# Picked experts' tiles in one line of pairs behind the last scan, with shifted rows and rings of eight

## The reference, cut to what matters

```
def step(S, inps):
    rt, kt, vt, dt = inps
    kv = kt[..., :, None] * vt[..., None, :]
    o = jnp.einsum('bhk,bhkv->bhv', rt, S + u[None, :, :, None] * kv)
    S = dt[..., None] * S + kv
    return (S, o)
...
up_r = jnp.einsum('th,reh->tre', xt, routed_up)
act = jax.nn.gelu(up_r, approximate=False) * gate[:, :, None]
routed = jnp.einsum('tre,rhe->th', act, routed_down)
```

## Time and profile before

| what | value |
|---|---|
| median of 3 runs | 5062.5 us |
| the profiled execution, its own time | 5088.27 us |
| span of its trace | 5086.5 us |
| mean granted TensorE clock (share of full speed) | 0.899 |
| busy: TensorE, VectorE, ScalarE, GpSimd | 4041.3, 3733.9, 2719.0, 3369.3 us |

### The profile page before, as it was taken

The page is one execution under the profiler, slowest core; times in us unless marked ns, Lnnn a source line. Parts: engine busy times, 40 slices in busy tenths (PEclk is TensorE's granted clock), DMA queues, the critical chain, the costliest instruction groups (busy, mean ns, idle before and its releaser), DMA issues. The chain is left out here.

```text
span 5086.5 us, 64064 instructions
## 1 busy us (share of the span) xinstructions
PE 4041.3 (79%) x19024; PEld 2762.4 (54%) x19024; DVE 3733.9 (73%) x6383; ACT 2719.0 (53%) x5646; POOL 3369.3 (66%) x2370
## 2 busy tenths in 40 slices
PE   5777787887778887878448989888888888489994
PEld 1344554565445654556345555555555555368883
DVE  6888698678886888741008998988889888645677
ACT  1333643454345543546237777777777777245552
POOL 3456576576566766672358888888888888645552
PEclk7888887999889988989679999999999999699997
DMA  4233445444544446641662122221112211396788
GB/s 180 85 102 127 145 134 134 143 146 132 134 146 144 156 129 151 167 154 53 144 152 84 59 68 83 84 72 70 65 67 82 85 67 66 136 237 206 243 279 279
DMA packets 378773, 659.74 MB, mean 130 GB/s; under 512 B 43616, under 2 KB 235488, under 8 KB 368096
## 3 DMA queue, kind: packets, MB, share of 16 engines
q1 hardware_dynamic: 288576, 464.59, 28.7%
q0 software_dynamic: 89856, 191.05, 13.4%
HBM read 455.29 MB, written 250.25 MB: 139 GB/s over the span
## 5 line engine op out<-in xcount | busy, mean ns | idle before, releaser
L1687 POOL TENSOR_TENSOR c_dbx<-c_dtx,c_Brep 128x1024 f32<-128x1024 f32 x512 | 1202.5, 2364 | 183.2 <-DVE c_hs L1705 99.0
L1705 DVE TENSOR_TENSOR_SCAN c_hs<-psum,c_carry,c_dbx 128x512 f32<-128x512 f32 x768 | 937.3, 1266 | 120.0 <-ACT psum L1694 70.7
L1116 POOL TENSOR_TENSOR a_kv<-a_rk,a_kv 128x512 f32<-128x512 f32 x512 | 708.1, 1391 | 431.2 <-DMA a_kv<-v_rows 419.7
L1125 DVE TENSOR_TENSOR_SCAN a_S<-a_decay,a_carry,a_kv 128x513 f32<-128x513 f32 x512 | 804.2, 1571 | 153.3 <-POOL a_kv L1116 147.8
L1694 ACT ACTIVATE psum<-c_dt,c_cols 128x512 f32<-128x512 f32 x1024 | 697.2, 688 | 364.9 <-DVE c_hs L1705 359.2
L1721 PEld LDWEIGHTS psum<-ident,c_hs 128*128 128x128 f32 x4096 | 488.1, 144 | 392.2 <-DVE c_hs L1705 213.8
L1721 PE MATMUL psum<-ident,c_hs 128*128 128x128 f32 x4096 | 611.0, 283 | 108.9 <-DVE c_hs L1705 104.1
L962 POOL DMA_INDIRECT picked_results<-a_t_y,a_to_slot x336 | 386.8, 1151 | 421.4 <-ACT a_t_y L953 165.8
L1131 DVE TENSOR_TENSOR a_prod<-a_rk,a_S 128x512 f32<-128x512 f32 x512 | 454.9, 888 | 78.3 <-PE psum L1147 78.3
L2110 POOL DMA_INDIRECT results<-d_ys,d_to_row x320 | 312.0, 975 | 250.4 <-issue 140.0
L872 POOL DMA_INDIRECT picked_rows<-a_row,a_to_row x256 | 351.8, 1374 | 122.7 <-issue 42.5
(11 more groups left out here) (316 smaller groups left out, 8161.6 us busy)
## 6 DMA issues: line engine op xcount, KB each, us to landing
a_kv<-v_rows SPq DMA_DIRECT2D x512, 256.0 KB
c_Brep<-b_rows SPq DMA_DIRECT2D x64, 1024.0 KB, 4.8
a_t_rows<-picked_rows SPq DMA_DIRECT2D x336, 144.0 KB
d_xs<-sorted_rows SPq DMA_DIRECT2D x320, 128.5 KB
x<-picked_results POOLq DMA_DIRECT2D x64, 512.0 KB, 7.6
d_w<-results SPq DMA_DIRECT2D x64, 512.0 KB, 11.4
d_w<-in_d_experts SPq DMA_DIRECT2D x32, 768.0 KB
picked_rows<-in_picked_pad SPq DMA_DIRECT2D x80, 144.0 KB
```

What stands on the lines that cost most here:

```text
L1116: m_kv[g] = pool.mark(nc.gpsimd.tensor_tensor(kv[:, g % NV, 1:C + 1], rk[slot][:, 1, hb, :], kv[:, g % NV, 1:C + 1], ALU.mult))
L1125: m_scan[q] = dve.mark(nc.vector.tensor_tensor_scan(S[:, q % NS, :], decay[cq % 2][:, hb, :], kv[:, q % NV, :], carry[:, sq_:sq_ + 1], ALU ...
L1687: m_dbx[g] = m_dbx[g + 1] = pool.mark(nc.gpsimd.tensor_tensor(dbx[:, r:r + 2, :], dtx[slot][:, e, :].unsqueeze(1).broadcast_to([P, 2, C]), ...
L1705: m_scan[q] = dve.mark(nc.vector.tensor_tensor_scan(hs[:, q % NR, :], psum[:, DA + q % ND, :], dbx[:, q % NX, :], first, ALU.mult, ALU.add))
```

## The change

- **Tiles.** SEGMENTS is [8, 8], so there are 2 × 144 = 288 tiles. None is computed during the scans. After the last scan `pairs_of_tiles` writes 144 pairs in one straight line: pair s is transposed, pair s-1 goes through the up weights, pair s-2 through the second transpose and the down weights. Each of the four TensorE steps has one PSUM bank of its own, the two copies out of PSUM and the copy of gates and slots are VectorE's, the Gelu and the scaling stay on ScalarE. What is left of layer 0 and `opening()` are background, one stage of each stream at each of two pauses a pair.
- **Combine.** The chunks of the first segment are combined in the tail, two chunks abreast, once its 72 pairs are done. Those of the second segment are combined during layer 1's scans; layer 1 waits for a chunk only where it loads it, and for the last tile stores before its scans.
- **Scans.** k, v and decay are stored one column late, in tiles of 513 columns whose column 0 comes from the chunk before (three small ScalarE copies a chunk), so a scan has 512 elements. `carry` is copied by ScalarE. The rings of kv, S and prod hold 8, 8 and 8 (before 6, 4 and 6), v is fetched LEAD = 5 steps ahead (3), and PACE is 3200 (4400).

```
-        NV, NS, NP = 6, 4, 6
-        kv, S, prod = brief("kv", [P, NV, C + 1]), brief("S", [P, NS, C + 1]), brief("prod", [P, NP, C])
+        NV, NS, NP = 8, 8, 8
+        kv, S, prod = brief("kv", [P, NV, C]), brief("S", [P, NS, C]), brief("prod", [P, NP, C])
...
+            if c >= 1:
+                act.after(*scanned, *m_done["ready", c - 1])
+                act.mark(nc.scalar.copy(decay[slot][:, :, 0], decay[1 - slot][:, :, C]))
+                m_edge = act.mark(nc.scalar.activation(ks[slot][:, :, 0], ks[1 - slot][:, :, C], ACT.Copy, scale=chunk_mask[:, c:c + 1]))
...
-        CHAIN_RATE, BEFORE_RATE, NORM_RATE, SORT_RATE, LEAD = 3, 1.3, 1.5, 1.0, 3
-        PACE = 4400
+        CHAIN_RATE, BEFORE_RATE, NORM_RATE, SORT_RATE, LEAD = 3, 1.3, 1.5, 1.0, 5
+        PACE = 3200
...
-                    m_kv[g] = pool.mark(nc.gpsimd.tensor_tensor(kv[:, g % NV, 1:C + 1], rk[slot][:, 1, hb, :], kv[:, g % NV, 1:C + 1], ALU.mult))
+                    m_kv[g] = pool.mark(nc.gpsimd.tensor_tensor(kv[:, g % NV, :], ks[slot][:, hb, 0:C], kv[:, g % NV, :], ALU.mult))
...
-                    dve.after(m_scan[q])
-                    m_kept[q] = dve.mark(nc.vector.tensor_copy(carry[:, q % steps - 3:q % steps + 1], S[:, q % NS - 3:q % NS + 1, C]))
+                    act.after(m_scan[q], m_start[0])
+                    m_kept[q] = act.mark(nc.scalar.copy(carry[:, q % steps - 3:q % steps + 1], S[:, q % NS - 3:q % NS + 1, C - 1]))
...
-    SEGMENTS = [2, 3, 4, 4, 3]
+    SEGMENTS = [8, 8]
```

The straight line, and what runs beside it (`left.advance_all()` pulls one stage of each background stream):

```
+            for s in range(total + 2):
+                if s < total:
+                    rows_turned(s)
+                if s >= 2:
+                    hidden_turned(s - 2)
+                pause()
+                if 1 <= s <= total:
+                    up(s - 1)
+                if s >= 2:
+                    down(s - 2)
+                    if s - 1 in begins:
+                        m_done["tiles", segment[s - 2]] = s - 1
+                if s + AHEAD < total:
+                    fetch(s + AHEAD)
+                pause()
...
+        for i in range(2):
+            left.streams.append([1.0, 0.0, [combine(c) for c in range(i, opens[-1], 2)]])
+        tail_done = [("plan", len(Z.SEGMENTS) - 1), ("scattered", last), ("out", last), ("final", 0)]
+
+        def pause():
+
+            now[0] += 1
+            left.advance_all()
+            if is_done(*tail_done) and not is_done("second"):
+                m_done["second"] = True
+                left.streams[3][2].append(second_layer(wait_summed, wait_left, [FD.freed[0], *G.freed[0:2]], [combine(c) for c in range(opens[-1], NCH)]))
```

365 lines of the change are left out of this document (153 added, 212 removed).

## The result

The changed kernel takes 5105.8 us (median of 4 runs, 5099.9 to 5106.7) where the kernel before takes 5063.2 in the same session (a set of runs timed together). The ratio is 1.0086, with a 95% interval of 1.0068 to 1.0104: slower by 43 us. The forecast was 4954 us, its range 4830 to 5090, and slower had a chance of 0.15. The profiled execution took 5099.9 us.

The account below looks back on a forecast made before the run. VectorE was taken to set the scans' pace, with tiles costing time through TensorE and GpSimd. Scans -260, tail +136 and layer 1 +15 gave -109 us, so 4954 us against the median 5062.5; range 4830 to 5090.

Parts of the forecast that it names:

- the third chunk: Layer 0 scans of the kernel before: a chunk in which no tile runs, 132 us, VectorE busy 108.2.
- No tiles. The chunk falls to what the third chunk shows: 132 us.: Layer 0 scans: without tiles beside them, each chunk takes 132 us, the base for the other scan terms.
- the range 110 to 132: Layer 0 scans: bounds around the forecast 122 us a chunk, the lower one with no wait left.
- carry to ScalarE, -1.9.: Layer 0 scans: 8 carry copies a chunk leave VectorE, -1.9 us; ScalarE's added waits priced at 0.
- Rings and lead, -6.1.: Layer 0 scans: larger rings remove the product's wait for TensorE's sum, -6.1 us a chunk; longer lead priced at 0.
- PACE, -4, bounds 0 and 17.7.: Layer 0 scans: TensorE reaches small products earlier, taking 4 of VectorE's other 17.7 us idle from a chunk.
- I add 2: Layer 0 scans: 2 us a chunk added because VectorE's idle time partly goes into longer scans.
- The tail, 418 + 87 + 36 + 30.: Between layers' scans: 144 pairs at 2.9 us, other TensorE work, combine and ends; 571 us against 435, +136.
- Layer 1, +15.: Layer 1 scans: a third of some 45 us of accumulating DMAs on GpSimd shows, +15 us, bounds 0 and 45.
- The first: Layer 0 scans: VectorE's gaps fill with collisions with GpSimd's products, 132 us a chunk, 5103 us; chance 0.15.
- The second rival: Tail: pairs no faster than the groups were, 3.26 us a pair, combine bursts held longer, 5041 us; chance 0.12.
- The third: Layer 0 scans: they reach VectorE's floor, 110 us a chunk, 4774 us; chance 0.08.

Follow-up runs that it names:

- e9: Kernel before with SEGMENTS 7, 5, 4 and a ring of 4 for fetched tile rows, so chunks 3 to 7 scan without tiles: 132.5 us a chunk.
- e3: Changed kernel with all old scan settings (rings 6, 4, 6, LEAD 3, PACE 4400, carry on VectorE): 138.9 us a chunk, ratio to kernel before 1.0329.
- e5: Changed kernel with five instead of three banks in the shared PSUM ring during the scans: 128.6 us a chunk, ratio to kernel before 1.0159.
- e11: Changed kernel with carry's copy back on VectorE: 129.9 us a chunk, one run.
- e7: Changed kernel with old rings (6, 4, 6) and LEAD 3 only: 128.7 us a chunk, ratio to kernel before 1.0160.
- e8: Changed kernel with PACE back at 4400 only: 139.6 us a chunk, ratio to kernel before 1.0434.
- e10: Changed kernel unedited, timed again in another session: 129.6 us a chunk, ratio to kernel before 1.0208.
- e4: Changed kernel with the second accumulating DMA in combine six stages after the first instead of three: 5085.0 us, ratio to kernel before 1.0048.
- e1: Changed kernel with GpSimd's product k * v replaced by a memset, so GpSimd only writes: 111.9 us a chunk, 4824.6 us, one run.
- e2: Changed kernel with decay and r copied to one PSUM bank each for scan and product: 121.7 us a chunk, 4971.4 us, ratio to kernel before 0.9823.
- e6: Changed kernel with all old scan settings and five banks in the shared PSUM ring: 135.5 us a chunk, ratio to kernel before 1.0341.
- e13: Changed kernel with all old scan settings, five banks and an empty turn after each feed_forward and shared step: 133.2 us a chunk, one run.

## Why the prediction was wrong

**What bounds the kernel.** Right: VectorE set the pace and does so now, at 115.3 of 129.5 us. The reading of the third chunk was right as well (e9).

**"No tiles. The chunk falls to what the third chunk shows: 132 us."** This step failed, and by the order of the prediction's own sum (first the move, then the settings) it is most of the scans' miss. The changed code at the old settings takes 138.9 us (e3), 6.9 more. The edit that took the tiles out of the scans also took two banks from the shared ring (3.4 us) and the empty turns between the steps of the feed-forward (2.3 to 3.3 us). Neither has a term in the sum. In the kernel as it was changed they may cost less: there the two banks are worth 1.0 us (e5), and the turns were not tried. That the new pace does part of the same work fits this, but is not shown. I had listed banks and block_work as things that moved, not as things that cost; of the range 110 to 132, the upper end was the base itself, so no cost on this side was covered at all.

**carry to ScalarE, -1.9.** Measured -0.3 (e11), at the new pace. The copies left VectorE (busy -1.5), and most of it came back as idle (+1.2).

**Rings and lead, -6.1.** Measured +0.9 (e7), at the new pace. The product's wait went, but PACE alone removes it; the scan's wait that the rings do take away turns into longer instructions.

**PACE, -4, bounds 0 and 17.7.** Measured -10.0 (e8): mis-sized, inside its bounds. Most of the idle time went, and not only the 4 us of it that I had put down to this.

**"I add 2" for longer scans.** Too small: with all settings together busy time rose by 3.5 to 3.8 us a chunk (111.8 to 115.3 or 115.6) although carry's 1.9 had left, so the rest grew by over 5. The settings together are worth 9.3 of the 10 forecast, by a sum of terms of which each was wrong: that this sum nearly came out is luck.

Thirteen chunks at 7.5 us are 98 us; the first takes 108.8 for 106, the second 116.9 for 122 and the last 107.2 for 122, and so the scans missed by 80.

**The tail, 418 + 87 + 36 + 30.** A pair takes 2.91 us in the first profile, so 418 was right there. In e10, which by its last phase is like the profile that the forecast stood on, pairs alone take 3.52, above even my upper bound of 3.26; so the reading that ScalarE's copies held a pair at 3.26 is not borne out there, and what held it stays open. The work beside the pairs is 61 + 43 = 104 for 87, the combining stretch 66 to 71 for 36 (e4's later DMA made the tail 25 shorter), and the ends 35 + 13 = 48 for 30. These make the 65 us in the first profile; the two first stretches, where pairs are slower, make another 59 in e10.

**Layer 1, +15.** Right: 12.5.

**The rivals.** The first gave 5103 us, and 5105.8 was measured. That the two agree is luck: it had the scans 70 us too long (2086 for 2016.5) and the tail 65 too short. Its mechanism was there (e1, e2), but it did not decide. With all 32 products apart VectorE would be busy for 130 us a chunk; it is busy for 115, and scan and product take 82 us a chunk, under the 95 that the prediction gave as a sign of being wrong. The same mechanism with the same instructions was in the kernel before. Its chunk without tiles was busy for 109.6 us (e9), carry's 1.9 among them, so at most 7.6 us a chunk of it are new, over 5 of them with the new settings, against 2 in my sum. The second rival, pairs no faster than groups, was right of e10's session (3.52, no faster than 3.26) and wrong of the first (2.91). The third, VectorE's floor at 110, was far: even without any collision (e1) the chunk is 111.9, since the waits rise.

**The range.** 5105.8 lies 16 us above it. The upper end took in part of one rival, and no term for what the new code itself may cost. In e10's session the changed kernel took 5197.4 us, far outside.

## What to carry to other kernels

When a change takes work out of a stage, a stretch in which that work happened not to run shows the stage without the work, but not without the code around it: ask what the removed code still did when it had nothing to do (a turn in a loop, a pace) and what the new layout took away (banks, buffers). Where VectorE with two SBUF inputs runs beside a GpSimd that reads SBUF, an idle microsecond that you remove on VectorE may come back as longer instructions: here larger rings removed 4 us of idle and added 5 of busy time (e7), while a smaller portion of work on TensorE's queue removed 12 and added 2 (e8). Moving one input of scan and product to PSUM removed their collisions themselves (1625 to 1272 ns, 947 to 662, e2). When VectorE waits shortly for TensorE, look at how large a portion of other work stands ahead in TensorE's queue: here one number in the pacing gave 10 us a chunk, and all rings gave nothing.

## What the runs showed that I had not expected

- Contention with GpSimd's product costs 29 us of VectorE's busy time in a chunk of 129.5 (e1), 22% of it, of which 17.6 us are time of the chunk: the scan 1625 against 1276 ns, the product 947 against 665. The mixes of the inputs pay as well: the mean of L457 is 1087 ns in the changed kernel and 744 ns in e1.
- The same program differs between sessions by more than its runs in one session do: the changed kernel 5105.8 and 5197.4 us, the kernel before 5061.1 to 5103.0, with scans and layer 1 equal. The ratio between two kernels moved with it, from 1.0086 to 1.0208. A forecast that rests on one profile takes over the state of its session.
- TensorE's granted clock in chunks 3 to 15 is 0.78 at PACE 4400 (e3, e8) and 0.81 to 0.82 at 3200, with TensorE busy 99.8 and 91 to 92 us a chunk (1297.51 and 1183.93 / 13): the same matmuls, in smaller portions, at a higher mean clock. At PACE 4400 it is 0.78 with three banks and with five (e3, e6) and 0.81 with five banks and the empty turns (e13): what the banks gave came without the clock. What part of PACE's 10 us is the clock's was not separated.
